# Two routed expert layers: bias term behind the last block, low parts of weights behind the slots, gates of the choices inside the block loop

## The reference, cut to what matters

```
h = gelu(einsum('td,edh->teh', x, w1) + b1)        # 512 -> 256
expert_out = einsum('teh,ehd->ted', h, w2) + b2    # 256 -> 512
combined = einsum('ted,te->td', expert_out, gate)  # gate: 0 outside the chosen experts
```

## Time and profile before

| what | value |
|---|---|
| median of 3 runs | 1212.32 us |
| lowest and highest run | 1208.69, 1212.51 us |
| the profiled execution | 1207.77 us |
| its span (first to last instruction) | 1205.4 us |
| mean granted TensorE clock | 0.85 of full speed |
| busy, TensorE matmuls | 857.3 us, 71% |
| busy, VectorE | 645.3 us, 54% |
| busy, GpSimd | 583.5 us, 48% |
| busy, ScalarE | 410.3 us, 34% |
| TensorE busy between 412 and 448 us | 27.06 us of 36 |
| TensorE busy between 1092 and 1124 us | 26.38 us of 32 |

### The profile page before, as it was taken

How to read it: one execution, slowest core, us unless ns; L and a number is a source line. 1 busy time by engine, 2 the same in 40 slices (tenths; PEclk the granted TensorE clock), 3 DMA queues, 4 the chain that set the end, 5 groups by cost and what they waited for, 6 DMA issues and landing times.

```text
span 1205.4 us, 13123 instructions
## 1 busy us (share of the span) xinstructions
PE 857.3 (71%) x4216; PEld 674.6 (56%) x4216; DVE 645.3 (54%) x1291; ACT 410.3 (34%) x664; POOL 583.5 (48%) x386
## 2 busy tenths in 40 slices
PE   3176779900198679942978988899999987736980
PEld 2165558800176348931867766677777766522870
DVE  4544433000266954437252257678787786796547
ACT  0111112100244515522221204666565665532450
POOL 1378788888312025510162214668677765531340
PEclk9977779955599659975989988999999999965895
DMA  9722331222785414452321104001010050153334
GB/s 274 136 22 19 21 36 1 0 0 0 170 232 190 176 53 141 152 188 75 127 61 44 35 35 110 22 19 53 18 27 1 19 157 0 71 201 102 115 117 148
DMA packets 78730, 101.48 MB, mean 84 GB/s; under 512 B 29120, under 2 KB 51904, under 8 KB 77136
## 3 DMA queue, kind: packets, MB, share of 16 engines
q1 hardware_dynamic: 51856, 76.52, 20.5%
q0 software_dynamic: 26816, 24.20, 11.3%
HBM read 65.50 MB, written 31.00 MB: 80 GB/s over the span
## 4 chain that ended last, share of the span: by engine, by line
PE 43%; DVE 22%; POOL 16%; DMA 9%; issue 7%; ACT 3%; SPq 0%; DVEq 0%; POOLq 0%; ACTq 0%
PE PS L296 27%; POOL edge_table L547 15%; DMA edge_table<-count,index 5%; PE PS L1770 3%; PE PS L1785 3%; DVE neg_max L1381 3%; PE PS L1759 2%; DVE APL L937 2%; PE PS L1784 2%; PE PS L1609 2%; DMA edge_table<-zeros 2%; PE PS L1637 1%; DVE XN L970 1%; DVE W2L L937 1%; DMA CT<-edge_table 1%
## 5 line engine op out<-in xcount | busy, mean ns | idle before, releaser
L547 POOL DMA_INDIRECT edge_table<-count,index x136 | 217.2, 1597 | 85.3 <-issue 37.3
L631 POOL TENSOR_SCALAR AP__176<-AP__176,rden 128x1024 f32<-128x1024 f32 x64 | 182.0, 2847 | 86.5 <-DVE rden L1386 85.9
L559 POOL CAST WH<-RAW 128x512 fp32r<-128x512 f32 x30 | 23.0, 767 | 165.3 <-PE PS L296 95.5
L1381 DVE TENSOR_REDUCE neg_max<-PS 128x1 f32<-128x1024 f32 x64 | 78.2, 1222 | 37.1 <-PE PS L1759 36.1
L663 ACT ACTIVATE APH<-PS 128x512 fp32r<-128x512 f32 x128 | 71.7, 597 | 70.2 <-PE PS L1770 45.6
L937 DVE TENSOR_TENSOR APL<-PS,APH 128x512 fp32r<-128x512 f32 x128 | 82.8, 678 | 23.7 <-ACT APH L663 23.6
L296 PE MATMUL PS<-XTH,WH 128*128 128x512 f32 x224 | 88.0, 442 | 6.4 <-DVE XTL L937 6.4
L583 POOL DMA_INDIRECT BX<-normalised,gather_i x38 | 38.0, 1000 | 108.9 <-DVE scatter_i L1223 84.2
L296 PE MATMUL PS<-XTL,WH 128*128 128x512 f32 x224 | 84.2, 425 | 0.0
L296 PE MATMUL PS<-XTH,WL 128*128 128x512 f32 x224 | 81.8, 413 | 0.0
L1770 PE MATMUL PS<-ident,AP__176 128*128 128x128 f32 x512 | 71.1, 281 | 11.6 <-DVE APL L937 10.8
(11 more groups left out here) (261 smaller groups left out, 2328.1 us busy)
## 6 DMA issues: line engine op xcount, KB each, us to landing
edge_table<-zeros SPq DMA_DIRECT2D x2, 4096.0 KB, 22.9
YT<-expert_rows SPq DMA_DIRECT2D x12, 512.0 KB, 6.6
CT<-edge_table SPq DMA_DIRECT2D x8, 512.0 KB, 6.0
CT<-edge_table POOLq DMA_DIRECT2D x8, 512.0 KB, 7.1
counts<-CT SPq DMA_DIRECT2D x8, 512.0 KB, 6.8
W1R<-in_L_ffn_w SPq DMA_DIRECT2D x8, 512.0 KB, 7.8
W2R<-in_L_ffn_w SPq DMA_DIRECT2D x8, 512.0 KB, 5.6
normalised<-XN SPq DMA_DIRECT2D x2, 2048.0 KB, 8.6
```

Source lines behind the costliest of these rows:

```text
L547: gp.indirect_dma_start(out=tables[r], out_offset=bass.IndirectOffsetOnAxis(ap=index[:, c:c + 1], axis=0), in_=count[:, c:c + 1], in_offse ...
L631: gp.tensor_scalar(AP_[:, i % 4, :], AP_[:, i % 4, :], rden[:, i % 4:i % 4 + 1], None, ALU.mult).then_inc(B["norm"], 1)
L1381: v.tensor_reduce(out=neg_max[:, i % 4:i % 4 + 1], in_=banks(2 * (i % 2)), axis=X_AXIS, op=ALU.max, negate=True).then_inc(B["mx"], 1)
```

## The change

Four pieces of text move. (1) TensorE's transposes of `gates` and all eight bias rows, ScalarE's copy to `gatesT` and VectorE's eight adds go behind the last block, with the wait for `xn_saved` and for the last adds; TensorE no longer waits for the adds ahead of the blocks. (2) The rest of the low parts goes from behind `hidden_bias(0)` to directly behind the slots. (3) In layer 0 the steps that make `gate_of` go into the block loop, three of them behind block 2 and three behind block 3. (4) On SP `results(1)` goes ahead of the wait for the adds, since these now come after it. TensorE's wait for the last `y_sb` of layer 0 moves from ahead of the graph convolution to ahead of the bias rows, and exists in layer 1 too.

```diff
@@ SP
         expert_biases("L1_ffn_b1")
+        results(1)
         wait(M["acc"], 2 * NT)
         sp.dma_start(g2_row[:, :], a["L1_ffn_g2"].partition_broadcast(P)).then_inc(rows1_in, 16)
-        results(1)
@@ ScalarE, moe
             for e in range(3, 6):
                 w2_hi(e)
-            act.wait_ge(M["gt_ps"], 2 * which + 2)
-            copy(gatesT[0:NEXP, :], PS[0:NEXP, 4:6, :].rearrange("p a b -> p (a b)"), M["gt"])
             for e in range(6, NEXP):
                 w2_hi(e)
...
             out_rows(n - 1)
+            act.wait_ge(M["gt_ps"], 2 * which + 2)
+            copy(gatesT[0:NEXP, :], PS[0:NEXP, 4:6, :].rearrange("p a b -> p (a b)"), M["gt"])
@@ VectorE, moe, behind scatter_i
-            v.wait_ge(M["xn_saved"], 16 * which + 16)
-            for t in range(NT):
-                v.wait_ge(M["g_ps"], which * NT + t + 1)
-                v.tensor_tensor(acc[:, t, :], acc[:, t, :], PS[:, (4 + t) % 8, :], ALU.add).then_inc(M["acc"], 1)
-            v.wait_ge(M["acc"], which * NT + NT)
+            weights_lo(len(tasks))
...
             hidden_bias(0)
-            weights_lo(len(tasks))
             v.wait_ge(M["gates"], which + 1)
-            if which == 0:
-                for c in range(2):
-                    step(v.tensor_tensor(chosen[:, :, :], gtmp[:, :, :], wide(place1[:, c, :]), ALU.is_equal))
-                    step(v.tensor_tensor(chosen[:, :, :], chosen[:, :, :], gates[:, :, :], ALU.mult))
-                    step(v.tensor_reduce(out=gate_of[:, c, :], in_=chosen[:, :, :], axis=X_AXIS, op=ALU.add))
+            def gate_of_choice(c):
+...
             for b in range(nb):
...
+                if which == 0 and 2 <= b < 4:
+                    gate_of_choice(b - 2)
+            v.wait_ge(M["xn_saved"], 16 * which + 16)
+            for t in range(NT):
+                v.wait_ge(M["g_ps"], which * NT + t + 1)
+                v.tensor_tensor(acc[:, t, :], acc[:, t, :], PS[:, (4 + t) % 8, :], ALU.add).then_inc(M["acc"], 1)
+            v.wait_ge(M["acc"], which * NT + NT)
@@ TensorE, moe
-            pe.wait_ge(M["gates"], which + 1)
-            for t in range(NT):
-                got = pe.transpose(PS[0:NEXP, 4 + t // 4, (t % 4) * P:(t % 4 + 1) * P], gates[:, t, :], ident[:, :])
-            got.then_inc(M["gt_ps"], 1)
...
-            bias_rows(6)
...
             pe.wait_ge(M["routed"], routed(which, "scatter"))
-            bias_rows(7)
-            pe.wait_ge(M["acc"], which * NT + NT)
...
+            pe.wait_ge(M["gates"], which + 1)
+            for t in range(NT):
+                got = pe.transpose(PS[0:NEXP, 4 + t // 4, (t % 4) * P:(t % 4 + 1) * P], gates[:, t, :], ident[:, :])
+            got.then_inc(M["gt_ps"], 1)
+            pe.wait_ge(M["gt"], 3 * which + 3)
+            pe.wait_ge(M["y_sb"], first + nb)
+            for t in range(NT):
+                pe.matmul(PS[:, (4 + t) % 8, :], gatesT[0:NEXP, t * P:(t + 1) * P], b2[:, which, :],
+                          start=True, stop=True).then_inc(M["g_ps"], 1)
@@ TensorE, behind layer 0
-        pe.wait_ge(M["y_sb"], BLOCKS[0])
```

More of the change, by code:

```diff
@@ L1258, in moe @@
             hidden_bias(0)
-            weights_lo(len(tasks))
             v.wait_ge(M["gates"], which + 1)
-            if which == 0:
-                for c in range(2):
-                    step(v.tensor_tensor(chosen[:, :, :], gtmp[:, :, :], wide(place1[:, c, :]), ALU.is_equal))
-                    step(v.tensor_tensor(chosen[:, :, :], chosen[:, :, :], gates[:, :, :], ALU.mult))
-                    step(v.tensor_reduce(out=gate_of[:, c, :], in_=chosen[:, :, :], axis=X_AXIS, op=ALU.add))
-            assert steps[0] == STEPS[0] + which * STEPS[1], steps
+            def gate_of_choice(c):
+                step(v.tensor_tensor(chosen[:, :, :], gtmp[:, :, :], wide(place1[:, c, :]), ALU.is_equal))
+                step(v.tensor_tensor(chosen[:, :, :], chosen[:, :, :], gates[:, :, :], ALU.mult))
+                step(v.tensor_reduce(out=gate_of[:, c, :], in_=chosen[:, :, :], axis=X_AXIS, op=ALU.add))
             for b in range(nb):
@@ L1274, in moe @@
                     v.tensor_tensor(X[:, b - 2, :], X[:, b - 2, :], row0[:, :], ALU.add).then_inc(F["beta"], 1)
+                if which == 0 and 2 <= b < 4:
+                    gate_of_choice(b - 2)
+            assert steps[0] == STEPS[0] + which * STEPS[1], steps
+            v.wait_ge(M["xn_saved"], 16 * which + 16)
[3 more added lines that the diff above has]
+            v.wait_ge(M["acc"], which * NT + NT)
             added, stats_before = [2 * NT * which], (2, 5)[which] * (2 * NT + 4)
```

## The result

| | before | after |
|---|---|---|
| median (4 runs each) | 1212.07 us | 1197.17 us |
| lowest and highest | 1208.69, 1212.51 | 1196.38, 1199.28 |
| the profiled execution | 1207.77 us | 1196.38 us |
| its span | 1205.4 us | 1194.6 us |
| mean granted TensorE clock | 0.85 | 0.86 |

The ratio is 0.9886, 95% interval [0.9864, 0.9908]: 1.1% faster. I had forecast 1205.9 us with a range down to 1197.5. The direction was right, the gain was 2.3 times as large as I said, and the time lies 0.3 us under the range. Between the two profiled executions the difference is 11.4 us; my sum said 6.4.

What follows compares the result with a forecast made beforehand. Bias rows, their adds and low parts delayed the first block, while VectorE idled behind the last. Gains of 8.65 and 8.3 us less tails of 3.7 and 6.85 gave 6.4 us, so 1205.9 us, range 1197.5 to 1211.5.

Steps and rivals of the forecast that it cites:

- The slots: Ahead of the first block, VectorE reads the slots 5.15 us earlier in layer 0 and 7.75 us in layer 1.
- Gathers under low parts: Ahead of the first block, each GpSimd gather takes 0.9 us more while VectorE's low parts run beside it.
- (b): Gathers get no turn until low parts end, 1211.1 us; or all bias rows at half clock, 1210.5; chance 0.15 together.
- Gates of the choices: Six steps of 0.26 us go into layer 0's block loop and cost nothing, covered by VectorE's 1.48 us wait.
- The clock: Full speed comes 1.7 us behind the first `out_rows` in both layers; together nothing, bounds 1.7 us either way.
- The tails: Behind the last block, the moved bias work loses 3.7 us in layer 0 and 6.85 us in layer 1.
- The sum: Over both expert layers, 8.65 + 8.3 + 0 - 3.7 - 6.85 = 6.4 us gained.
- The median: The profiled execution, forecast at 1201.4 us, lies 4.5 us under the median, which gives 1205.9 us.
- (a): Behind the last block, bias rows keep full speed: 2.3 us lost in place of 10.55, 1197.7 us; chance 0.13.
- (c): The clock rises late in the block loops; 15 us later in both layers gives 1220.9 us; chance 0.07.
- (d): Something unseen delays `out_rows(0)`, half the gain ahead of the blocks goes: 2.05 us lost, 1214.4 us; chance 0.05.

Runs made afterwards that it cites:

- low_back: The changed kernel with the rest of the low parts back behind `hidden_bias(0)`, gate steps left in the loop; 1196.81 us (one run).
- bias_alone: The changed kernel with the low parts and the six gate steps back in their old places, so only the bias term moves; 1198.80 us, ratio 0.9920.
- split_again: The kernel of `split` unchanged, run once more beside the padded ones; 1188.67 us, ratio 0.9835.
- split: The changed kernel with gate transposes, copy and four bias rows ahead of the first block, four rows behind the last; 1186.66 us, ratio 0.9835.
- tall: The changed kernel with its bias products at full height, 128 rows in place of 8, on other data; 1191.23 us (one run).
- no_bias: The changed kernel without the term of the second biases (no transposes of the gates, copy, products or adds); 1187.33 us, ratio 0.9805.
- gt_front: The changed kernel with only the transposes of the gates and their copy back at the front; 1197.19 us, ratio 0.9888.
- pad: The kernel of `split` with every bias product made full height, 128 rows, all but 8 zeros; 1185.25 us, ratio 0.9818.
- pad1: The kernel of `pad` with one more full-height product ahead of the first transposes of layer 0; 1184.87 us, ratio 0.9812.

## Why the prediction was right and wrong, by its own steps

- **The slots: right.** Said 5.15 and 7.75 us earlier, measured 5.27 and 7.84.
- **Gathers under low parts: right.** Said 0.9 us more each, measured 0.8 to 1.0 (1.78 to 1.93 against 0.95). They get their turn, so that half of rival (b) was wrong. `hidden(0)` was said to come 23.6 us after the first step of the gates, and came at 23.48. The Trainium skill, SBUF — State Buffer, section Who interferes with whom, says that a VectorE instruction with two SBUF inputs contends with a GpSimd instruction that reads SBUF. The trace agrees with the direction: these low parts have both inputs in SBUF, and the gathers beside them took 0.8 to 1.0 us more.
- **Gates of the choices: right.** No cost in the loop, the wait behind them 0.91 us. Taking them out of the stop is worth 1.5 us.
- **The clock: this is the step that failed.** I said "I can't tell where it comes after the change and take the middle, 1.7 us behind the first `out_rows`, for both", which put the term at zero, with 1.7 us either way. In layer 1 that held: 7.6 us gained up to the last matmul, said 8.3 - 0.9 = 7.4. In layer 0 the rise came 3.1 us ahead of the first `out_rows`, 4.8 us earlier than I took it. Up to the last matmul 12.4 us were gained where I had 8.65 + 0.9, so the term was 2.9 us short, outside its own bounds. I had tied the rise to `out_rows`, which is a mark in the program, and read only the last rise of the kernel before. Its clock had been up from 10.8 to 14.2 us behind the first transposes, for most of which TensorE stood still. In its place the runs show two things. The fall at 14.2 and the 3.4 us of half speed behind it come with the stop ahead of `out_rows(0)` (`low_back`, `bias_alone`), and the change removed this stop. The first rise, 10.8 us before and 6.0 after, lies ahead of the stop. It was at 10.3 to 10.8 us in the three profiles with the stop and at 6.0 to 6.2 in seven without, but `split_again` had 10.0 without one. So why it came so early in layer 0 stays open, and a part of the 2.9 us may be luck.
- **The tails: right mechanism, too dear.** Said 3.7 + 6.85 = 10.55 us lost, measured 2.85 + 5.43 = 8.28. The bias rows start 1.98 us behind the last matmul (said 2.0) and are at half speed from the middle on, as I chose by rows. The fall came at 5.3 and 5.9 us and not at 4.2, 1.4 us later on average. Each us later gives back half a us: 0.55 + 0.85 = 1.4 of the 2.3. Counted at the records, the sixteen took 10.79 and 10.18 us where I had 11.4, together 1.8 us less, and the last add ended 0.7 us behind them where I had 0.9, in each layer.
- **The sum.** 6.4 + 2.9 (clock, layer 0) + 0.2 (layer 1) + 2.3 (tails) = 11.8, against 11.7 measured in the two stages.
- **The median.** I added 4.5 us because the profiled execution of before lay so far under its median. That of after lies 0.8 under its own. This is another 3.7 us of the 8.7 by which 1205.9 was off, more than the clock's 2.9. Two executions of one kernel differed by 9.5 us, 6.2 of them ahead of the first step of the gates (`split`, `split_again`), so such a distance can't be carried over to the changed kernel.
- **The rivals.** (a) didn't come, since products of 8 rows don't hold the speed. That the median lies 0.5 us from its 1197.7 is a coincidence. The second half of (b) didn't come either, as the first bias rows ran at full speed. (c) didn't come: the rise was 6 us behind the first transposes in layer 0, 12 in layer 1, 17.6 and 10.9 before. (d) was wrong: nothing else was late.

What stays open: which of the two rises a stage gets, near 6 or near 10 to 12 us behind the first transposes. In layer 1 the kernel with all bias rows at the back had 12.2, 12.2 and 12.4 in three profiles that have the low parts ahead, but `tall` and `no_bias`, the same up to there, had 6.0, and so did `low_back` and `bias_alone`. `split` had both. Nothing in the first blocks tells them apart. It is worth 2.3 us at the last matmul of layer 1 (76.8 against 74.5), so part of a difference of this size between two single profiles is chance.

## What to carry to other kernels

Work that is off the critical path can be put into a hole, but a hole is a number of us, and the work must be priced at the speed it will have there; here half of it fitted, and half at each end beat all at the back by 4 to 6 us. A stop of TensorE early in a stage costs its length and then once more, if it takes the granted clock away. When the profiled execution lies away from the median, give the distance to the range and not to the forecast.

## What the runs showed of the hardware

- TensorE products of 8 rows (8x128 by 8x512, float32) don't hold full speed, though the engine is busy without a pause: the clock fell 2.1 and 2.6 us behind the last full-height matmul (`gt_front`), no later than where nothing followed (3.2 to 5.3 us, before and `no_bias`), while full-height products of the same number of columns held it for their 7.1 us and 3 us beyond (`tall`). Rows of zeros counted towards it: the four products ahead of the first block brought full speed before it in both layers of `pad` and `pad1`, and in neither of `split` and `split_again`.
- A stop of 1.9 to 3.4 us soon after the rise brought half speed for another 3.4 us in each of the three profiles that had one (3.19 us in before, 3.37 in `bias_alone`, 1.86 in `low_back`).
- The place of the rise differed between two executions of one kernel by 4.0 and 6.4 us (`split`, `split_again`).
- A gather by GpSimd beside VectorE's subtractions with both inputs in SBUF takes 1.8 to 1.9 us in place of 0.95 (after, and every other kernel with the low parts there).
